# A recommendation tower on one core: TensorE raises its semaphores once for several results, and two looked-up features share a PSUM bank

## The chip, the cores and the metric

The kernel runs on one core of one Trainium2 chip. The metric is the device time of one launch in microseconds; the number given is the median of the runs. The engines are called as in the profile: PE (TensorE), PEld (its weight loads), DVE (VectorE), ACT (ScalarE), POOL (GpSimd) and SP (SyncE, which only issues transfers here).

## The reference, cut

2048 samples, 26 categorical features, vectors of 128 numbers.

```python
e = jnp.stack([tbl_f[ids[:, f]] for f in range(26)], axis=1)    # written out, feature by feature
combined = jnp.concatenate([dense[:, None, :], e], axis=1)       # 27 vectors a sample
interactions = jnp.einsum('bfd,bgd->bfg', combined, combined)
z = jnp.concatenate([dense, interactions[:, _IU0, _IU1]], axis=1)   # 128 + 351 pairs
h = jnp.concatenate([z, dense], axis=1)                          # 607
h = jnp.maximum(h @ W_top1 + b_top1, 0.0)                        # 607 -> 512
h = jnp.maximum(h @ W_top2 + b_top2, 0.0)                        # 512 -> 256
y = h @ W_top3                                                   # 256 -> 1
```

## The kernel before, in words

The batch is cut into 16 tiles of 128 samples, two tiles (`u` = 0 and 1) to a block `m`, 8 blocks (`LAST` = 7). Every engine runs its own hand-written program; semaphores alone set the order between them. Blocks 2 to 6 are a hardware loop, blocks 0, 1 and 7 are written out.

A block goes through these steps:

- **Gathers** (POOL, L372). For 18 of the features the 128 rows of a tile are fetched by one indirect DMA each, 18 in a row for a tile. They start when DVE has copied the tile's ids to `tile_ids` (L736), which it does in the middle of moving the tile before out of PSUM. The gathers for tile `u` of the next block therefore run while PE works on the dots of tile `u` of this one.
- **Look-ups** (`look_up_products`, L406). The other 8 features have 1000-row tables that stay in SBUF. DVE makes a one-hot matrix of 8 chunks for a feature and both tiles (`make_one_hots`, L723, `HOT` = 3 buffers), PE multiplies it with the table in a high and a low part: 16 matmuls of 256 columns for a feature, into bank `looked_up[n % 2]`. ACT copies the result out (L564, L566) and raises `product_copied`. PE raises `half_used` after 8 matmuls and `product_done` after 16; DVE refills the first half of a one-hot buffer after the one and the second half after the other.
- **Turns** (`turn_tile`, L427). 19 transposes of a tile in 5 groups, each group to a bank of its own, `turned_done` raised after each. DVE copies groups 0, 2, 4 (L739), ACT groups 1, 3 (L580).
- **Dots** (`dot_tile`, L445). 8 fills of 4 products each (8 matmul records a fill), in three banks in turn: fill `b` may start when fill `b` - 3 has been copied out. ACT copies each fill (L591) when `dots_done` says so. Below they are called fill 0 to fill 7; fills 2 and 5 go to the bank named `turned`.
- The dots go to DRAM and come back by pair (SP).
- **Layers**. Layer 1 has 4 outputs `o` of 12 matmuls (L465) in two banks; DVE adds the bias and applies the maximum (`relu_layer1`, L773), ACT and DVE split the result in a high and a low part. Layer 2 has 2 outputs of 12 matmuls (L498, L783), layer 3 is small (L508, L790). `layer_done` is raised after each output and once for layer 3.

PE's order in a steady block is: turn tile 0, layer 2 of two blocks ago, dots of tile 0, layer 3, the 8 look-ups for the next block, turn tile 1, output 0 of layer 1 of the block before, dots of tile 1, outputs 1 to 3. In the last block there are no look-ups and no gathers, and its own layer 1 goes to four banks (`last_layer1`, L483). In the first block, ACT makes the high part of table `n` + 3 only after it has copied feature `n` out.

Of the kernel before, what the change touches and what calls it, by code (L numbers as in the profile page):

```python
# [1 line left out]

# [8 lines left out]
P = 128  # L32
# [5 lines left out]
COLS = PER_BLOCK * P  # L38
# [4 lines left out]
LAYER1, LAYER2 = H1 // P, H2 // P  # L43
# [6 lines left out]
N_ROW, N_PRODUCT = len(ROW_FEATURES), len(PRODUCT_FEATURES)  # L50

SLOT_VECTORS = [0] + [f + 1 for f in ROW_FEATURES] + [f + 1 for f in PRODUCT_FEATURES]
PRODUCT_SLOT = 1 + N_ROW
TABLE_ROWS = 1000
CHUNKS = -(-TABLE_ROWS // P)
ROWS_K = TABLE_ROWS // CHUNKS
ROWS_SPRAY = ROWS_K - ROWS_K % 16
HOT = 3
# [9 lines left out]
N_GROUPS = len(GROUPS)  # L68
# [4 lines left out]
FILLS = QUADS // PER_BANK  # L73
# [8 lines left out]
K_TILES = 1 + PAIRS // K_PAIRS  # L82
SCRATCH_STORES = 2 * IN_QUAD
HIDDEN_LOADS = K_TILES - 1
WEIGHT_LOADS = 7
WEIGHT_SPLITS = 3
SPLIT_AFTER = 5

# [15 lines left out]
def build(nc, dense, ids, ids_by_feature, tables, W1, b1, W2, b2, W3, y):  # L104
    with ExitStack() as ctx:
# [10 lines left out]
        def sem(name):  # L116
            return ctx.enter_context(nc.semaphore(name))
# [8 lines left out]
        whole_tables, parts = sb_split("tables", [P, N_PRODUCT, CHUNKS, D])  # L126
# [3 lines left out]
        combined = sb("combined", [P, PER_BLOCK, P, VECTORS])  # L130
# [3 lines left out]
        ahead = sb("ahead", [P, N_PRODUCT, P])  # L134
# [66 lines left out]
        gathered = [[sem(f"gathered{u}_{g}") for g in range(N_GROUPS)] for u in range(PER_BLOCK)]  # L201
        dense_loaded = [sem(f"dense_loaded{u}") for u in range(PER_BLOCK)]
        one_hot_ready = sem("one_hot_ready")
        half_used = sem("half_used")
        product_done = sem("product_done")
        product_copied = sem("product_copied")
        ahead_moved = sem("ahead_moved")
# [19 lines left out]

        ids_by_tile = ids.rearrange("(p t) f -> p t f", t=TILES)
        dense_by_tile = dense.rearrange("(p t) d -> p t d", t=TILES)

        def tile_columns(ap, u):

# [159 lines left out]
        def _(pe):  # L392
            def look_up_products(m, first):

                for n in range(N_PRODUCT):

                    pe.wait_ge(one_hot_ready, m * N_PRODUCT + n + 1)
                    if first:

                        pe.wait_ge(table_split, n + 1)  # L400
                    if n >= 2:

                        pe.wait_ge(product_copied, m * N_PRODUCT + n - 1)
                    for c in range(CHUNKS):
                        for part in (HIGH, LOW):
                            last = nc.tensor.matmul(looked_up[n % 2][:, 0:COLS], parts[part][0:ROWS_K, n, c, :],  # L406
                                                    one_hot[0:ROWS_K, n % HOT, c, :],
                                                    start=(c == 0 and part == HIGH),
                                                    stop=(c == CHUNKS - 1 and part == LOW))
                        if c == CHUNKS // 2 - 1:  # L410
                            last.then_inc(half_used, 1)
                    last.then_inc(product_done, 1)

            def turn_tile(m, u, products, first=False):
                if not first:

                    pe.wait_ge(dots_copied, (m * PER_BLOCK + u) * FILLS)

                pe.wait_ge(dense_loaded[u], (m + 1) * 16)
                for g, slots in enumerate(GROUPS):  # L420
                    if g == 2:

                        pe.wait_ge(product_copied, products)

                    pe.wait_ge(gathered[u][g], (m + 1) * 16 * (len(slots) - (g == 0)))
                    for q, slot in enumerate(slots):
                        last = nc.tensor.transpose(group_bank[g][:, q * P:(q + 1) * P], rows[:, u, slot, :], identity[:])  # L427
                    last.then_inc(turned_done, 1)

            def dot_tile(m, u):  # L430

                pe.wait_ge(even_copied, (m * PER_BLOCK + u + 1) * EVEN_GROUPS)
                pe.wait_ge(odd_copied, (m * PER_BLOCK + u + 1) * ODD_GROUPS)
                if u == 0:
                    pe.wait_ge(product_copied, (m + 1) * N_PRODUCT)
                else:
                    pe.wait_ge(ahead_moved, m + 1)
                for b in range(FILLS):
                    if b >= DOT_BANKS:

                        pe.wait_ge(dots_copied, m * DOT_FILLS + u * FILLS + b - DOT_BANKS + 1)
                    for q in range(PER_BANK):
                        at = (b * PER_BANK + q) * IN_QUAD
                        quad = combined[:, u, at:at + IN_QUAD, :].rearrange("d j s -> d (j s)")
                        last = nc.tensor.matmul(dot_bank[b % DOT_BANKS][0:SQUARE, q * SQUARE:(q + 1) * SQUARE], quad, quad,  # L445
                                                start=True, stop=True)
                    last.then_inc(dots_done, 1)

            def layer1(n, first, outs=range(LAYER1)):

                pe.wait_ge(dense_kept, n + 1)
                if first:

                    pe.wait_ge(weights_split, WEIGHT_SPLITS)
                for o in outs:
                    if not first or o >= 2:

                        pe.wait_ge(layer_copied, n * LAYERS + max(0, o - 1))
                    for k in range(K_TILES):
                        if k > 0 and o == 0:  # L460

                            pe.wait_ge(pairs_split, n * HIDDEN_LOADS + k)
                        rows_k = P if k == 0 else K_PAIRS
                        for w, x in PART_PAIRS:
                            last = nc.tensor.matmul(mlp_bank[o % 2][:, 0:COLS], w1[w][0:rows_k, k, o * P:(o + 1) * P],  # L465
                                                    hidden0(x, rows_k, k), start=(k == 0 and w == x),
                                                    stop=(k == K_TILES - 1 and w == LOW))
                    last.then_inc(layer_done, 1)

            def last_layer1(tiles):  # L470

                if tiles[0] == 0:

                    pe.wait_ge(dense_kept, BLOCKS)
                    pe.wait_ge(dots_copied, BLOCKS * DOT_FILLS)
                for o in range(LAYER1):
                    for k in tiles:
                        if k > 0 and o == 0:

                            pe.wait_ge(pairs_split, LAST * HIDDEN_LOADS + k)  # L480
                        rows_k = P if k == 0 else K_PAIRS
                        for w, x in PART_PAIRS:
                            last = nc.tensor.matmul(last_bank[o][:, 0:COLS], w1[w][0:rows_k, k, o * P:(o + 1) * P],  # L483
                                                    hidden0(x, rows_k, k), start=(k == 0 and w == x),
                                                    stop=(k == K_TILES - 1 and w == LOW))
                    if tiles[-1] == K_TILES - 1:
                        last.then_inc(layer_done, 1)

            def layer2(n):

                pe.wait_ge(layer_copied, n * LAYERS + LAYER1 - 1)
                for o in range(LAYER2):
                    for k in range(LAYER1):
                        if o == 0:

                            pe.wait_ge(hidden1_split, n * LAYER1 + k + 1)
                        for w, x in PART_PAIRS:
                            last = nc.tensor.matmul(mlp_bank[o % 2][:, 0:COLS], w2[w][:, k, o * P:(o + 1) * P],  # L498
                                                    hidden1[x][:, k, :], start=(k == 0 and w == x),
                                                    stop=(k == LAYER1 - 1 and w == LOW))  # L500
                    last.then_inc(layer_done, 1)

            def layer3(n):

# [54 lines left out]
        def _(act):  # L559
            def copy_products(m, features=range(N_PRODUCT)):  # L560
                for n in features:

                    act.wait_ge(product_done, m * N_PRODUCT + n + 1)
                    nc.scalar.copy(combined[:, 0, :, PRODUCT_SLOT + n], looked_up[n % 2][:, 0:P])  # L564

                    nc.scalar.copy(ahead[:, n, :], looked_up[n % 2][:, P:COLS]).then_inc(product_copied, 1)  # L566

            def move_ahead(m, products):

# [125 lines left out]
        def _(dve):  # L695
# [8 lines left out]
            def make_one_hots(m, n, first):  # L704
# [10 lines left out]
                    dve.wait_ge(product_done, m * N_PRODUCT)  # L715
                for c in range(CHUNKS):
                    if n >= HOT and c == 0:

                        dve.wait_ge(half_used, m * N_PRODUCT + n - HOT + 1)
                    if n >= HOT and c == CHUNKS // 2:  # L720

                        dve.wait_ge(product_done, m * N_PRODUCT + n - HOT + 1)
                    last = nc.vector.tensor_scalar(one_hot[:, n % HOT, c, :], of,  # L723
                                                   chunk_row[:, c:c + 1], None, ALU.is_equal)
# [159 lines left out]
```

## Time and profile before

| | |
|---|---|
| median of 3 runs | 691.15 us (689.26 to 691.96) |
| span of the profiled execution | 677.5 us |
| outside the span, against the median | 13.65 us |
| PE busy | 423.8 us, 63% of the span |
| DVE, ACT, POOL busy | 239.6, 170.0, 275.0 us |
| matmuls | 2992 |
| gathers on POOL | 288, 273.7 us |

The page gives no time of its own for the profiled execution but the span, so the part outside it is counted against the median. Start times of PE's instructions are recorded; their ends are modelled. A release marked "remote" or "another core or an unknown queue" is one for which the profile found no instruction that ended just before: on one core, here, it means that the semaphore came long after the instruction that raises it had started.

### The profile page before, as it was taken

What the parts mean: (1) busy time and instruction counts of PE and PEld (TensorE: products, weight loads), DVE (VectorE), ACT (ScalarE), POOL (GpSimd) and SP (SyncE); (2) the same over time, 40 slices, a digit from 0 to 9 for tenths busy, and PEclk for the clock granted to TensorE, in tenths of its full rate; (3) what the DMA queues carried; (4) which work ended last, traced back from release to release, by engine and by line L of the source; (5) the groups of instructions that cost most, each with busy time, mean ns of one, the idle gap of its engine ahead of it and who ended that gap; (6) DMA issues with size and microseconds to landing.
All of it is one profiled execution on the core that took longest, in us unless ns stands there. A gap on an engine that the chain in (4) does not pass through costs nothing.

```text
span 677.5 us, 8517 instructions
## 1 busy us (share of the span) xinstructions
PE 423.8 (63%) x2992; PEld 403.1 (59%) x2992; DVE 239.6 (35%) x700; ACT 170.0 (25%) x366; POOL 275.0 (41%) x297
## 2 busy tenths in 40 slices
PE   2525354856947279471795726957269571784997
PEld 2415253855946179471794726956269471783997
DVE  5725210762504335043260432603434052530334
ACT  2204120431314024030231401313023040230551
POOL 6771737054172701727017271172712727036000
PEclk9967676786986659766597665976679575896899
DMA  8930211431114311243012430124301152001440
GB/s 222 275 93 14 71 31 50 83 108 43 51 52 83 90 29 44 55 86 87 15 48 53 81 92 12 54 51 81 94 28 48 52 99 74 19 23 50 85 64 23
DMA packets 61247, 46.01 MB, mean 68 GB/s; under 512 B 45677, under 2 KB 51301, under 8 KB 61228
## 3 DMA queue, kind: packets, MB, share of 16 engines
q1 hardware_dynamic: 52012, 26.87, 17.8%
q0 software_dynamic: 9216, 18.89, 10.8%
q8 instruction: 12, 0.20, 0.1%
q14 instruction: 7, 0.06, 0.0%
HBM read 37.20 MB, written 8.53 MB: 67 GB/s over the span
## 4 chain that ended last, share of the span: by engine, by line
PE 49%; another core or an unknown queue 34%; issue 11%; ACT 2%; DMA 2%; DVE 2%; SPq 1%; ACTq 0%; DVEq 0%
PE looked_up L406 20%; PE dot_bank L445 9%; PE mlp_bank L465 7%; PE mlp_bank L498 3%; PE turned L427 3%; PE turned L445 3%; PE looked_up L427 2%; DMA whole_tables<-in_tbl 2%; PE mlp_bank L508 1%; ACT dots L591 1%; PE dot_bank L427 1%; DVE whole_hidden L773 1%; ACT high_tables L635 1%; DVE combined L739 0%
## 5 line engine op out<-in xcount | busy, mean ns | idle before, releaser
L372 POOL DMA_INDIRECT rows<-in_tbl,tile_ids x288 | 273.7, 950 | 347.0 <-DVE tile_ids L736 262.4
L406 PE MATMUL looked_up<-one_hot,high_tables 125*128 125x256 f32 x512 | 144.0, 314 | 46.0 <-issue 23.4
L445 PE MATMUL dot_bank<-combined 128*108 128x108 f32 x768 | 99.4, 287 | 77.9 <-issue 41.8
L406 PE MATMUL looked_up<-one_hot,low_tables 125*128 125x256 f32 x512 | 141.6, 310 | 8.1 <-issue 8.1
L723 DVE TENSOR_SCALAR one_hot<-spread_ids,chunk_row 128x256 fp32r<-128x256 int32 x448 | 126.5, 359 | 52.6 <-remote 42.2
L406 PEld LDWEIGHTS looked_up<-one_hot,high_tables 125*128 125x128 f32 x512 | 113.0, 221 | 49.0 <-issue 49.0
L445 PEld LDWEIGHTS dot_bank<-combined 128*108 128x108 f32 x768 | 90.3, 197 | 84.1 <-issue 46.0
L406 PEld LDWEIGHTS looked_up<-one_hot,low_tables 125*128 125x128 f32 x512 | 112.7, 220 | 8.9 <-issue 8.9
L591 ACT COPY dots<-dot_bank 108x432 f32<-108x432 f32 x96 | 49.3, 519 | 242.3 <-remote 151.7
L773 DVE TENSOR_SCALAR whole_hidden<-mlp_bank,bias 128x256 f32<-128x256 f32 x28 | 13.5, 481 | 161.5 <-remote 99.1
L445 PE MATMUL turned<-combined 128*108 128x108 f32 x256 | 33.8, 281 | 47.2 <-issue 47.2
L445 PEld LDWEIGHTS turned<-combined 128*108 128x108 f32 x256 | 30.3, 194 | 48.2 <-issue 48.2
L564 ACT COPY combined<-looked_up 128x128 f32<-128x128 f32 x64 | 27.1, 423 | 118.4 <-PE looked_up L406 88.2
L465 PE MATMUL mlp_bank<-low_hidden,high_w 128*128 128x256 f32 (+1 forms) x112 | 40.4, 361 | 18.4 <-issue 18.4
L465 PEld LDWEIGHTS mlp_bank<-low_hidden,high_w 128*128 128x128 f32 (+1 forms) x112 | 29.1, 259 | 22.4 <-issue 22.2
L591 ACT COPY dots<-turned 108x432 f32<-108x432 f32 x32 | 16.6, 520 | 98.5 <-remote 85.5
L790 DVE COPY y_sb<-mlp_bank 128x2 f32 (+1 forms) x8 | 1.3, 159 | 112.8 <-PE mlp_bank L508 112.8
L465 PE MATMUL mlp_bank<-high_pairs,high_w 117*128 117x256 f32 x84 | 29.0, 346 | 13.3 <-issue 13.2
L465 PE MATMUL mlp_bank<-high_pairs,low_w 117*128 117x256 f32 x84 | 29.7, 354 | 10.2 <-issue 9.8
L427 PE MATMUL turned<-identity,rows 128*128 128x128 f32 x128 | 22.7, 337 | 13.8 <-ACT dots L591 13.8
L723 DVE TENSOR_SCALAR one_hot<-first_ids,chunk_row 128x256 fp32r<-128x256 int32 x64 | 19.8, 379 | 27.7 <-remote 20.8
L465 PEld LDWEIGHTS mlp_bank<-high_pairs,low_w 117*128 117x128 f32 x84 | 21.9, 261 | 12.0 <-issue 11.9
(73 smaller groups left out, 451.9 us busy)
## 6 DMA issues: line engine op xcount, KB each, us to landing
spread_ids<-in_ids_by_feature SPq DMA_DIRECT2D x28, 256.0 KB
scratch<-dots SPq DMA_DIRECT2D x28, 208.0 KB
rows<-in_tbl,tile_ids POOLq DMA_INDIRECT x288
whole_tables<-in_tbl SPq DMA_DIRECT2D x8, 448.0 KB
whole_hidden<-scratch SPq DMA_DIRECT2D x24, 117.0 KB
scratch<-dots SPq DMA_DIRECT2D x28, 52.0 KB
rows<-in_r_dense_features SPq DMA_DIRECT2D x16, 64.0 KB
first_ids<-in_ids_by_feature SPq DMA_DIRECT2D x1, 896.0 KB, 8.5
```

The lines of the kernel that those rows point to most:

```text
L372: nc.gpsimd.indirect_dma_start(rows[:, u, slot, :], None, tables[f][:, :], bass.IndirectOffsetOnAxis(ap=tile_ids[:, u, slot - 1:slot], axi ...
L406: last = nc.tensor.matmul(looked_up[n % 2][:, 0:COLS], parts[part][0:ROWS_K, n, c, :], one_hot[0:ROWS_K, n % HOT, c, :], start=(c == 0 and ...
L427: last = nc.tensor.transpose(group_bank[g][:, q * P:(q + 1) * P], rows[:, u, slot, :], identity[:])
L445: last = nc.tensor.matmul(dot_bank[b % DOT_BANKS][0:SQUARE, q * SQUARE:(q + 1) * SQUARE], quad, quad, start=True, stop=True)
L465: last = nc.tensor.matmul(mlp_bank[o % 2][:, 0:COLS], w1[w][0:rows_k, k, o * P:(o + 1) * P], hidden0(x, rows_k, k), start=(k == 0 and w == x),
L498: last = nc.tensor.matmul(mlp_bank[o % 2][:, 0:COLS], w2[w][:, k, o * P:(o + 1) * P], hidden1[x][:, k, :], start=(k == 0 and w == x), stop ...
L508: last = nc.tensor.matmul(mlp_bank[0][:, u:u + 1], hidden2[:, k, u, :], w3[:, k:k + 1], start=(k == 0), stop=(k == LAYER2 - 1))
L564: nc.scalar.copy(combined[:, 0, :, PRODUCT_SLOT + n], looked_up[n % 2][:, 0:P])
L591: nc.scalar.copy(dots[0:SQUARE, :, at:at + PER_BANK], dot_bank[b % DOT_BANKS][0:SQUARE, 0:PER_BANK * SQUARE].rearrange("p (q c) -> p c q", ...
L635: nc.scalar.copy(parts[HIGH][0:ROWS_K, n, :, :], whole_tables[0:ROWS_K, n, :, :]).then_inc(high_part_made, 1)
L723: last = nc.vector.tensor_scalar(one_hot[:, n % HOT, c, :], of, chunk_row[:, c:c + 1], None, ALU.is_equal)
L773: nc.vector.tensor_scalar(whole1[:, o, :], banks[o][:, 0:COLS], bias1[:, o:o + 1], 0.0, ALU.add, ALU.max).then_inc(layer_copied, 1)
```

## The change

No instruction is added, removed or moved on any engine. What changes is which matmuls raise a semaphore, by how much, and what waits for it:

- turns: `turned_done` is raised after group 1 (by 2) and after group 4 (by 3), no longer after each of the 5 groups;
- dots: `dots_done` is raised by 2 after every second fill (1, 3, 5, 7);
- look-ups: two features share a bank, in its two halves of 256 columns, so that the two banks hold four features. `product_done` is raised by 2 after the second of a pair. PE waits for `product_copied` once for a pair, and then for the pair two before. `half_used` is gone, and DVE waits for `product_done` ahead of the whole one-hot;
- layer 1: `layer_done` is raised by 2 after outputs 1 and 3; the last block's by 4 after output 3;
- layer 2: by 2 after output 1.

Every wait of ACT, DVE and SP keeps its count, so a waiter for the first of a pair now waits for the second. What order PE works in, the three banks of the dots and the three one-hot buffers stay.

```diff
+LOOKS_PER_BANK = 2
+TURNED_SIGNALS = {1: 2, N_GROUPS - 1: N_GROUPS - 2}
+DOTS_SIGNALS = {b: 2 for b in range(1, FILLS, 2)}
...
+        def look_view(n):
+            at = n % LOOKS_PER_BANK * COLS
+            return looked_up[n // LOOKS_PER_BANK % 2][:, at:at + COLS]
...
-                    if n >= 2:
-                        pe.wait_ge(product_copied, m * N_PRODUCT + n - 1)
+                    if n >= 2 * LOOKS_PER_BANK and n % LOOKS_PER_BANK == 0:
+                        pe.wait_ge(product_copied, m * N_PRODUCT + n - LOOKS_PER_BANK)
...
-                        if c == CHUNKS // 2 - 1:
-                            last.then_inc(half_used, 1)
-                    last.then_inc(product_done, 1)
+                    if n % LOOKS_PER_BANK == LOOKS_PER_BANK - 1:
+                        last.then_inc(product_done, LOOKS_PER_BANK)
...
-                    last.then_inc(turned_done, 1)
+                    if g in TURNED_SIGNALS:
+                        last.then_inc(turned_done, TURNED_SIGNALS[g])
...
-                    last.then_inc(dots_done, 1)
+                    if b in DOTS_SIGNALS:
+                        last.then_inc(dots_done, DOTS_SIGNALS[b])
...
-                    last.then_inc(layer_done, 1)
+                    if o % 2 == 1:
+                        last.then_inc(layer_done, 2)
...
-                    if tiles[-1] == K_TILES - 1:
-                        last.then_inc(layer_done, 1)
+                if tiles[-1] == K_TILES - 1:
+                    last.then_inc(layer_done, LAYER1)
...
-                    last.then_inc(layer_done, 1)
+                last.then_inc(layer_done, LAYER2)
...
                 for c in range(CHUNKS):
                     if n >= HOT and c == 0:
-                        dve.wait_ge(half_used, m * N_PRODUCT + n - HOT + 1)
-                    if n >= HOT and c == CHUNKS // 2:
                         dve.wait_ge(product_done, m * N_PRODUCT + n - HOT + 1)
```

ACT's copies of the look-ups (L564, L566) read `look_view(n)` instead of `looked_up[n % 2]`.

## Rows read from the trace of the kernel before

**Rows 1.** The page: its head.

```profile
span 677.5 us, 8517 instructions
```

**Rows 2.** Waits: who waited for whom; us in total, times, longest.

```profile
ACT dots L591 <- remote: 237.2, 38, 14.2
...
DVE whole_hidden L773 <- remote: 99.1, 4, 24.9
```

**Rows 3.** Timeline, dots of tile 0: start, us, engine, what [idle before <- releaser].

```profile
216.80 0.94 POOL L372 DMA_INDIRECT rows<-in_tbl,tile_ids  x1 [11.44 <-DVE tile_ids L736]
...
220.00 1.91 PE L445 MATMUL dot_bank<-combined 128*108 128x108 f32 x16
...
228.93 0.52 ACT L591 COPY dots<-turned 108x432 f32<-108x432 f32 x1 [8.07 <-remote]
...
238.03 0.94 POOL L372 DMA_INDIRECT rows<-in_tbl,tile_ids  x1 [0.31 <-issue]
238.05 0.52 ACT L591 COPY dots<-dot_bank 108x432 f32<-108x432 f32 x1 [8.61 <-remote]
...
242.26 0.52 ACT L591 COPY dots<-dot_bank 108x432 f32<-108x432 f32 x1 [3.70 <-remote]
```

**Rows 4.** Timeline, dots of tile 1 and outputs 1 and 2 of layer 1.

```profile
352.79 0.94 POOL L372 DMA_INDIRECT rows<-in_tbl,tile_ids  x1 [29.50 <-DVE tile_ids L736]
...
353.09 0.48 DVE L773 TENSOR_SCALAR whole_hidden<-mlp_bank,bias 128x256 f32<-128x256 f32 x1 [0.65 <-PE mlp_bank L465]
...
359.04 1.01 PE L445 MATMUL dot_bank<-combined 128*108 128x108 f32 x8 [1.42 <-issue]
...
361.92 1.77 PE L445 MATMUL dot_bank<-combined 128*108 128x108 f32 x8 [1.87 <-issue]
...
366.08 0.41 PE L465 MATMUL mlp_bank<-high_dense,high_w 128*128 128x256 f32 x1
...
367.01 0.35 PE L465 MATMUL mlp_bank<-low_hidden,high_w 128*128 128x256 f32 x1 [0.52 <-issue]
...
368.45 0.52 ACT L591 COPY dots<-turned 108x432 f32<-108x432 f32 x1 [6.58 <-remote]
...
373.99 0.94 POOL L372 DMA_INDIRECT rows<-in_tbl,tile_ids  x1 [0.30 <-issue]
...
377.59 0.52 ACT L591 COPY dots<-dot_bank 108x432 f32<-108x432 f32 x1 [8.63 <-remote]
...
378.26 0.37 PE L465 MATMUL mlp_bank<-high_pairs,low_w 117*128 117x256 f32 x1
...
378.49 0.48 DVE L773 TENSOR_SCALAR whole_hidden<-mlp_bank,bias 128x256 f32<-128x256 f32 x1 [24.91 <-remote]
```

**Rows 5.** Timeline, the end of the dots of tile 0, two blocks later.

```profile
405.01 1.78 PE L445 MATMUL turned<-combined 128*108 128x108 f32 x8 [11.69 <-issue]
...
412.17 0.94 ACT L591 COPY dots<-dot_bank 108x432 f32<-108x432 f32 x2 [7.22 <-remote]
...
412.74 3.22 PE L445 MATMUL dot_bank<-combined 128*108 128x108 f32 x16 [5.96 <-ACT dots L591]
```

**Rows 6.** The chain that ended last: start, us, what.

```profile
379.03 2.93 PE mlp_bank L465 x12
...
583.27 15.46 PE looked_up L406 x128
...
667.93 2.17 PE dot_bank L483 x18
671.00 2.64 PE mlp_bank L498 x18
```

**Rows 7.** Timeline, DVE in the look-ups: half a one-hot.

```profile
249.80 1.14 DVE L723 TENSOR_SCALAR one_hot<-spread_ids,chunk_row 128x256 fp32r<-128x256 int32 x4 [0.56 <-PE looked_up L406]
```

**Rows 8.** Timeline, DVE in the turn of tile 1.

```profile
436.28 0.69 DVE L739 COPY combined<-looked_up 128x512 f32<-128x512 f32 x1 [0.18 <-PE looked_up L427]
...
437.18 0.17 DVE L736 COPY tile_ids<-all_ids 128x18 int32 x1 [0.21 <-PE dot_bank L427]
```

More of the change, by code:

```diff
@@ L203, in build @@
         one_hot_ready = sem("one_hot_ready")
-        half_used = sem("half_used")
         product_done = sem("product_done")
@@ L400, in look_up_products @@
                         pe.wait_ge(table_split, n + 1)
-                    if n >= 2:
-                        pe.wait_ge(product_copied, m * N_PRODUCT + n - 1)
+                    if n >= 2 * LOOKS_PER_BANK and n % LOOKS_PER_BANK == 0:
+                        pe.wait_ge(product_copied, m * N_PRODUCT + n - LOOKS_PER_BANK)
                     for c in range(CHUNKS):
                         for part in (HIGH, LOW):
-                            last = nc.tensor.matmul(looked_up[n % 2][:, 0:COLS], parts[part][0:ROWS_K, n, c, :],
+                            last = nc.tensor.matmul(look_view(n), parts[part][0:ROWS_K, n, c, :],
                                                     one_hot[0:ROWS_K, n % HOT, c, :],
@@ L563, in copy_products @@
                     act.wait_ge(product_done, m * N_PRODUCT + n + 1)
-                    nc.scalar.copy(combined[:, 0, :, PRODUCT_SLOT + n], looked_up[n % 2][:, 0:P])
-                    nc.scalar.copy(ahead[:, n, :], looked_up[n % 2][:, P:COLS]).then_inc(product_copied, 1)
+                    nc.scalar.copy(combined[:, 0, :, PRODUCT_SLOT + n], look_view(n)[:, 0:P])
+                    nc.scalar.copy(ahead[:, n, :], look_view(n)[:, P:COLS]).then_inc(product_copied, 1)
             def move_ahead(m, products):
```

## The prediction

> **What bounds the kernel now.** I read the page first. The span is 677.5 us [rows 1] and PE, the busiest engine, works 63% of it, so a third of the time is waiting. The table of waits says where: ACT waits 38 times, 237.2 us in all, for the fills of the dots, and DVE 4 times, 99.1 us, for an output of layer 1 [rows 2]. Both wait for PE, and both rows say "remote": the semaphore came long after the matmul. So the next view is the timeline of the places where that happens.
>
> Tile 0 of a block: the gathers of POOL start at 216.80. PE starts the last matmuls of fills 3 and 4 from 220.00 and is through with them by 221.91. ACT receives fill 2 at 228.93, fill 3 at 238.05, fill 4 at 242.26. The last of the 18 gathers starts at 238.03 and ends at 238.97 [rows 3]. So while POOL gathers, PE's semaphores come up to 16 us late and some 9 us apart; 3.3 us after the last gather everything owed arrives at once. Tile 1 shows the same: gathers from 352.79 to 374.93, fill 5 received at 368.45, fill 6 at 377.59, although fills 6 and 7 were issued at 359.04 and 361.92 [rows 4].
>
> The question on which all hangs is what is slow: the semaphore, or every instruction of PE. Output 2 of layer 1 answers it. Its 12 matmuls run from 366.08 to 378.26, 12.2 us, where 12 of the same take 2.93 us in output 3 [rows 4, 6]. Eleven of these twelve raise no semaphore, and they wait for none. They do not come in bursts after a semaphore is let through; the second already waits 0.52 us for nothing that is seen [rows 4]. At 366.08 what PE has issued and not been acknowledged is fill 6, fill 7 and output 1, 8 + 8 + 12 matmuls, each with its weight load: 56 instructions, and the rest of fill 5. I read that as a queue of a fixed length, emptied in order at one rate for every instruction: the 16 instructions of fill 6 take 377.59 - 368.45 = 9.1 us, 0.57 us each; the 24 of output 2 take 12.2 us, 0.51 us each. The rate goes with the instruction, not with the semaphore.
>
> So each of the stretches is pinned at both ends: it starts with the gathers, and ends some 3 us after them, plus what is still to do then. There are 14 of them, two in each of blocks 0 to 6.
>
> **The change part by part.** Fewer semaphores do not shorten that queue, since all 2992 matmuls and their loads remain. What they do is to let waiters start later.
>
> *Output pairs of layer 1.* Now output 0 is received at 353.09, before the queue is full; bank 0 is free, and output 2 is done under the stretch's cover, so only output 3 is left at 379.03 [rows 4, 6]. After the change output 0 is told of together with output 1, at 378.49. Output 2 then waits for the bank and comes behind the stretch. It costs the time of 12 matmuls, 2.93 us less what of that is waiting [rows 6]; what is late next is the turn of tile 0, its copies, and through `tile_ids` the gathers. I take 2.4 us, six times (blocks 1 to 6): 14.4 us. Bounds: 0 if some other stretch swallows it, 2.9 us each, 17.4 us.
>
> *Fill pairs, tile 0.* Fill 5 needs fill 2 copied. Before, fill 2 is received ahead of the end and fill 5 runs at 405.01; fills 6 and 7 follow at 412.74 and take 3.22 us [rows 5]. After it, fill 2 is received with fill 3, at 412.17, and three fills of 1.6 us stand there instead of two: +1.6 us. Where fill 3 is received before the end, as at 238.05, fill 7 is held by fill 4 at 242.26 as before, and the cost is 0 [rows 3]. In the trace four of the five looped blocks look like the first case. I take 1.2 us, six times: 7.2 us; bounds 0 and 1.6 us each, 9.6 us. Tile 1 has the same waits, but there PE has outputs 1 and 2 to do under cover: 0.
>
> *Turns, tile 1.* Groups 2, 3 and 4 are told of together. DVE now copies group 2 at 436.28, while PE transposes, and `tile_ids` at 437.18 [rows 8]; after it, group 2 (0.69 us) comes first, so `tile_ids` and all 18 gathers start 0.65 us later, and the stretch ends that much later. Six times: 3.9 us. For tile 0 DVE is behind PE with its own work already: 0.
>
> *Look-ups.* PE takes 15.46 us for 128 matmuls, 1.93 us a feature [rows 6]; DVE makes half a one-hot in 1.14 us, some 2.1 us for a whole one when it does not stop [rows 7]. So DVE is the slower one, and only the three one-hots in store hide it. Before, it starts the fourth after half of feature 0, at about 1.0 us; 5 x 2.1 us later, at 11.5, the last is ready, and PE wants it at 13.5: hidden. After it, DVE starts the fourth only when features 0 and 1 are done, at 3.9 us; the last is ready at 3.9 + 5 x 2.1 = 14.4, and with the semaphores between at about 14.5: PE ends at 16.4 instead of 15.46, +1.0 us, and +1.2 where its clock is low at first. I take 1.1 us, six times: 6.6 us; bounds 0 and 1.9 us each (DVE at its slower rate beside gathers), 11.4 us. The wider banks take PE's wait for ACT's copies away; in the steady blocks it is not seen, so nothing is gained. In the first block they let feature 4 run early, but feature 5 then waits for its one-hot, which waits for features 2 and 3 together; both ways end after the gathers. I count 0, and 2.5 us for the two stretches of block 0 and the later copies.
>
> *The last block.* There are no gathers. Its layer 1 gives up all four outputs at once: DVE's four maxima of 0.48 us [rows 4] stand behind the last matmul instead of beside them, between 667.93 + 2.17 and 671.00 [rows 6]: about +1.4 us. The copy of fill 6, the wait of output 2 for output 0's maximum and layer 2's pair add 0.4, 0.65 and 0.65 us. Sum 3.1 us; bounds 1 and 5 us.
>
> *The semaphores themselves.* 128 matmuls with 16 raises among them are 0.121 us apart [rows 6], so a raise costs no time that I can see outside the stretches: 0. The Trainium skill (TensorE: Matmul & The Clock Gate, section "The cost: per-tile semaphore tail") speaks for the change: increments serialize, and each adds 26.3 ns. No row here shows it. By that rule alone the 233 raises removed (64 in the dots, 48 in the turns, 96 in the look-ups, 25 in the layers) would give back 6.1 us, and the time would be 685 us if nothing else happened.
>
> The sum is 14.4 + 7.2 + 3.9 + 6.6 + 2.5 + 3.1 = 37.7 us. The span becomes 715.2 us; with the 13.65 us outside it, 728.9 us: I say 729. All low bounds together give some 698 us, all high ones some 741 us.
>
> **The rivals.**
>
> *The semaphore is what is slow (faster).* If each raise is held up while POOL gathers, and the instructions only behind it, then half the raises are half the waiting. For it: the 38 waits of ACT come one by one with a fill, 6.2 us each [rows 2], and so does what the change removes. Against it: output 2, which crawls without raising anything [rows 4]. Price: 38 x 6.2 / 2 = 119 us back, less the 37.7 us: 691 - 119 + 38 = 610 us. It decides as soon as fill 3 is received some 9 us earlier than now.
>
> *The semaphore is slow, but the end of the stretch is set by the gathers (little change).* Then tile 0 ends with fill 7 already done, 5 us less in each of six blocks instead of 7.2 us more, but the other terms stay: 729 - 7 - 21 = 701 us.
>
> *The page's rule, with the losses hidden (slightly faster).* As a mechanism of this kernel: every later start of ACT and DVE falls into a wait that POOL sets anyway, output 2 included, and only the work around raises is saved. By rows this is bounded by 0 us: 691 us. With the rule of the skill (the section named above) it is 685 us.
>
> *The first block goes wrong (slower still).* ACT makes tables 5 to 7 only after a pair is received. If the pair of features 4 and 5 misses the burst after the gathers, or the signals come later by one more stretch of 9 us [rows 3], that is 9 us or more on top, 738 to 750 us.
>
> **How the numbers follow.** My forecast, with its own range 705 to 742, has 0.67; the first rival 0.13; the second 0.07; the third 0.08 (half of it faster, half within 0.5%); the fourth 0.05. The range 690 to 746 leaves out the first rival, part of the third and part of the fourth, together just under 0.2. Half a per cent is about what a measurement of this kernel can tell from no change. Faster: 0.13 + 0.04 and a little for what I don't see, 0.18. Same: 0.04 and the edge of the second, 0.06. Slower: 0.76.
>
> **What the profile after would show.** ACT's waits for the dots: four a tile, longer each, with the total near 237 us or above (right), or near half (first rival). The time from the last gather to the next burst stays 3 us. Behind it stand 24 matmuls of L465 in the chain instead of 12. The look-ups of a block take 16.5 to 18.5 us instead of 15.5 to 17.4, with DVE named as the releaser. `tile_ids` of tile 1 comes after a copy of 0.69 us. The prediction is wrong if outputs of layer 1 or fills are received while the gathers still run, in shorter steps than 9 us; then my reading of the queue has fallen.

## The result and the profile after

The changed kernel is slower: 721.8 us against 690.7 us, ratio 1.048 (95% interval 1.042 to 1.055). Two further sets gave 1.054 (1.048 to 1.061) and 1.055 (1.053 to 1.058). The range held, the direction and the size too: the sum was +37.7 us, and by their ratios the three sets show +33, +37 and +38 us.

One number of mine was wrong and cancels out. A run's time is its span and 1.8 us (731.26 us for a span of 729.5 us), not 13.65 us more. The profile of before, with a span of 677.5 us, stands for a run of 679.3 us: 1.7% below the median of 690.7 us, and below the lowest of the six runs behind it (684.5 us). As a ratio of spans the forecast was 715.2 / 677.5 = 1.056.

The page of the changed kernel, its head (answers to [rows 1]) and its waits (answers to [rows 2]):

```profile
span 729.5 us, 8489 instructions
...
PE 421.7 (58%) x2992; PEld 399.8 (55%) x2992; DVE 236.7 (32%) x700; ACT 160.7 (22%) x366; POOL 275.4 (38%) x297
```

```profile
ACT dots L581 <- remote: 284.8, 28, 21.0
DVE whole_hidden L760 <- remote: 156.5, 6, 26.1
```

ACT waits less often for the dots and longer in all: 28 times and 284.8 us, where it was 38 and 237.2. In a second profile of the changed kernel it is 26 times and 271.3 us. Half the raises did not halve the waiting. The work is the same, 2992 matmuls, and what was added is idle time. The two spans differ by 52 us, but only some 31 to 38 us of that are the change's: the profiled execution of the changed kernel was the slowest of its six runs, and that of before was a short one. The table by stages below therefore has further profiles beside these two.

Tile 1, the end of a stretch of the changed kernel (timeline; answers to [rows 4]):

```profile
399.76 0.94 POOL L359 DMA_INDIRECT rows<-in_tbl,tile_ids  x1 [0.30 <-issue]
404.06 0.94 ACT L581 COPY dots<-dot_bank 108x432 f32<-108x432 f32 x2 [11.74 <-remote]
404.18 0.88 DVE L760 TENSOR_SCALAR whole_hidden<-mlp_bank,bias 128x256 f32<-128x256 f32 x2 [26.02 <-remote]
404.72 0.58 PE L453 MATMUL mlp_bank<-high_dense,high_w 128*128 128x256 f32 x1 [8.41 <-DVE whole_hidden L760]
```

and the chain that ended last, the same place (answers to the first of [rows 6]):

```profile
404.72 5.44 PE mlp_bank L453 x24
```

The last gather ends at 400.70; 3.4 us later ACT gets fills 6 and 7, and DVE gets outputs 0 and 1 together. Behind the stretch stand 24 matmuls and 5.44 us, where 12 and 2.93 us stood. That step happened as told, in every block.

Tile 0 (timeline; answers to [rows 3] and [rows 5]):

```profile
415.06 0.94 POOL L359 DMA_INDIRECT rows<-in_tbl,tile_ids  x1 [14.35 <-DVE tile_ids L723]
...
426.51 0.52 ACT L581 COPY dots<-turned 108x432 f32<-108x432 f32 x1 [8.85 <-remote]
...
440.68 0.52 ACT L581 COPY dots<-dot_bank 108x432 f32<-108x432 f32 x1 [13.22 <-remote]
441.09 0.53 ACT L581 COPY dots<-turned 108x432 f32<-108x432 f32 x1
...
443.06 0.94 ACT L581 COPY dots<-dot_bank 108x432 f32<-108x432 f32 x2 [1.45 <-PE dot_bank L432]
```

Here I was wrong. Fill 3 comes with fill 2 at 11.4 us after the first gather, not at the burst, so fill 6 too is issued ahead of it, and only fill 7 is left behind it. The copy of the last fill starts 28.4 us after the first gather, where it was 29.4 in the block of [rows 5].

The look-ups (timeline of DVE, one block; answers to [rows 7]), ahead of them the same of the kernel before:

```profile
422.49 8.50 DVE L723 TENSOR_SCALAR one_hot<-spread_ids,chunk_row 128x256 fp32r<-128x256 int32 x32 [0.20 <-PE looked_up L406]
```

```profile
449.89 4.30 DVE L710 TENSOR_SCALAR one_hot<-spread_ids,chunk_row 128x256 fp32r<-128x256 int32 x16 [5.03 <-PE looked_up L393]
454.36 4.29 DVE L710 TENSOR_SCALAR one_hot<-spread_ids,chunk_row 128x256 fp32r<-128x256 int32 x16 [0.17 <-PE looked_up L393]
458.82 2.19 DVE L710 TENSOR_SCALAR one_hot<-spread_ids,chunk_row 128x256 fp32r<-128x256 int32 x8 [0.17 <-PE looked_up L393]
```

Before, DVE makes four one-hots in one run. After, it makes two, stops, and is let go by PE 4.46 us later each time: a one-hot (2.19 us) and the feature that uses it and completes the pair (2.18 us on its own) now stand in a row.

The turn of tile 1 (timeline; answers to [rows 8]) goes as forecast, group 2 and then the ids:

```profile
465.72 0.69 DVE L726 COPY combined<-looked_up 128x512 f32<-128x512 f32 x1 [0.88 <-PE dot_bank L413]
466.33 0.17 DVE L723 COPY tile_ids<-all_ids 128x18 int32 x1
```

**By stages.** The table is made from the timelines: from the first matmul of a stage to the first of the next, mean of blocks 2 to 6, in us. "More raises" is an experiment below whose time is that of before; it shows how far one profile differs from the next. Its block is 85.12 us and lies nearer to the usual run of before than the 83.76 us of the short profile.

| | turn 0 | layer 2 | dots 0 | layer 3 | look-ups | turn 1 | output 0 | dots 1 | outputs 1-3 | block |
|---|---|---|---|---|---|---|---|---|---|---|
| before | 3.25 | 2.95 | 27.23 | 1.37 | 16.68 | 2.00 | 1.51 | 10.45 | 18.32 | 83.76 |
| more raises (e9) | 2.96 | 2.95 | 27.92 | 1.60 | 17.23 | 1.99 | 1.51 | 12.93 | 16.04 | 85.12 |
| after | 2.08 | 2.95 | 28.46 | 1.45 | 18.83 | 2.37 | 1.77 | 15.72 | 15.77 | 89.40 |
| after, again | 2.09 | 2.96 | 27.84 | 1.60 | 18.70 | 2.37 | 1.76 | 15.56 | 16.04 | 88.91 |

Dots 1 and outputs 1 to 3 belong together: 28.8 and 29.0 us before, 31.5 and 31.6 after.

### The profile page after: what moved, and what is told of

Its sections match the earlier page's. It is cut to its first block, busy times and chain, and to the rows that moved or that the text cites. A ratio compares the mean times of both kernels' runs of the same rounds, so it can differ in the third digit from the quotient of the medians.

```text
span 729.5 us, 8489 instructions
## 1 busy us (share of the span) xinstructions
PE 421.7 (58%) x2992; PEld 399.8 (55%) x2992; DVE 236.7 (32%) x700; ACT 160.7 (22%) x366; POOL 275.4 (38%) x297
## 4 chain that ended last, share of the span: by engine, by line
another core or an unknown queue 42%; PE 34%; DVE 10%; issue 8%; ACT 3%; DMA 2%; SPq 1%; DVEq 0%; ACTq 0%
PE looked_up L393 13%; DVE one_hot L710 7%; PE dot_bank L432 6%; PE mlp_bank L453 5%; PE mlp_bank L488 3%; PE looked_up L413 2%; ACT dots L581 2%; PE turned L432 1%; PE mlp_bank L498 1%; DMA first_ids<-in_ids_by_feature 1%; PE turned L413 1%; DVE low_tables L691 1%; PE dot_bank L413 1%; DVE whole_hidden L760 1%
## 5 line engine op out<-in xcount | busy, mean ns | idle before, releaser
L393 PE MATMUL looked_up<-one_hot,high_tables 125*128 125x256 f32 x512 | 146.0, 317 | 45.5 <-DVE low_tables L691 22.6
L432 PE MATMUL dot_bank<-combined 128*108 128x108 f32 x768 | 101.2, 290 | 97.0 <-ACT dots L581 56.5
L393 PEld LDWEIGHTS looked_up<-one_hot,high_tables 125*128 125x128 f32 x512 | 111.1, 217 | 54.8 <-issue 44.1
L393 PEld LDWEIGHTS looked_up<-one_hot,low_tables 125*128 125x128 f32 x512 | 110.9, 217 | 9.2 <-issue 9.2
L581 ACT COPY dots<-dot_bank 108x432 f32<-108x432 f32 x96 | 46.8, 522 | 259.5 <-remote 201.9
L432 PE MATMUL turned<-combined 128*108 128x108 f32 x256 | 35.6, 289 | 89.2 <-issue 69.0
L760 DVE TENSOR_SCALAR whole_hidden<-mlp_bank,bias 128x256 f32<-128x256 f32 x28 | 12.9, 480 | 179.8 <-remote 156.5
L453 PE MATMUL mlp_bank<-high_dense,high_w 128*128 128x256 f32 x28 | 12.9, 462 | 50.5 <-DVE whole_hidden L760 50.5
L453 PEld LDWEIGHTS mlp_bank<-high_dense,high_w 128*128 128x128 f32 x28 | 7.6, 272 | 52.4 <-DVE whole_hidden L760 52.4
L453 PEld LDWEIGHTS mlp_bank<-low_hidden,high_w 128*128 128x128 f32 (+1 forms) x112 | 31.0, 277 | 0.0
L453 PE MATMUL mlp_bank<-high_pairs,high_w 117*128 117x256 f32 x84 | 30.5, 363 | 0.0
```

Of the source, the lines that this page charges most:

```text
L393: last = nc.tensor.matmul(look_view(n), parts[part][0:ROWS_K, n, c, :], one_hot[0:ROWS_K, n % HOT, c, :], start=(c == 0 and part == HIGH), ...
L581: nc.scalar.copy(dots[0:SQUARE, :, at:at + PER_BANK], dot_bank[b % DOT_BANKS][0:SQUARE, 0:PER_BANK * SQUARE].rearrange("p (q c) -> p c q", ...
L760: nc.vector.tensor_scalar(whole1[:, o, :], banks[o][:, 0:COLS], bias1[:, o:o + 1], 0.0, ALU.add, ALU.max).then_inc(layer_copied, 1)
```

## The experiments

The theory: while POOL gathers, what PE has finished is acknowledged late, in order, at a rate for each instruction; the end of such a stretch is set by the gathers; the change moves work out of its cover and starves PE of one-hots. The main rival: a raise is what is slow.

### One part at a time

Layer pairs alone (e1), fill pairs alone (e2), the look-ups alone (e3), the turns alone (e4). Before took 688.2 us beside them.

```diff
e1:  -                    last.then_inc(layer_done, 1)
     +                    if o % 2 == 1:
     +                        last.then_inc(layer_done, 2)      # last_layer1: LAYER1 at the end; layer2: LAYER2 at the end
e2:  -                    last.then_inc(dots_done, 1)
     +                    if b % 2 == 1:
     +                        last.then_inc(dots_done, 2)
e3:  look_view, the wait for product_copied by pairs, product_done by pairs, no half_used
e4:  -                    last.then_inc(turned_done, 1)
     +                    if g in (1, N_GROUPS - 1):
     +                        last.then_inc(turned_done, 2 if g == 1 else N_GROUPS - 2)
```

> The kernel before with the layer pairs alone (layer 1 after outputs 1 and 3, layer 2 after output 1, the last block's layer 1 after output 3). My theory (a queue at a rate per instruction, stretches pinned to the gathers): output 2 of layer 1 comes out of cover, some 2.4 us a block in blocks 1 to 6 (14.4 us) and 2.7 us at the end, so 17 us more, about +2.5%, and 24 matmuls instead of 12 behind each stretch of tile 1. Rival (a raise is what is slow while POOL gathers): fewer raises ahead of the burst, so 5 us or more less than before.

> The kernel before with the fill pairs of the dots alone. As predicted: +1.2 us a block in six blocks, +7 us (+1.0%). What the trace of the changed kernel suggests instead: nothing a block (28.6 against 28.7 us from the first gather to the end of the dots of tile 0), so within 3 us of before. Rival (a raise is slow): half the raises are half the waiting, 30 us or more less.

> The kernel before with the look-ups of the change alone (two features in a bank, product_done by pairs, no half_used). As predicted: DVE's later start costs 1.1 us a block, +6.6 us (+1.0%). The trace of the changed kernel suggests 2.15 us a block, +13 us (+1.9%), DVE the releaser of every second feature. Rival (raises are slow): 16 raises fewer 4 in a stage without gathers change nothing; in the first block they save up to 9 us.

> The kernel before with the turns raised twice alone. As predicted: tile_ids and with it the gathers of tile 1 start 0.65 us later in six blocks, +3.9 us (+0.6%). The trace of the changed kernel suggests 0.83 us for tile 1 and 0.16 for tile 0: +6 us (+0.9%). Rival: nothing, or a little less than before.

| part | predicted | ratio (95%) | us |
|---|---|---|---|
| e1 layer pairs | +17 | 1.012 (1.005 to 1.020) | +8.5 |
| e2 fill pairs | +7 | 1.006 (1.002 to 1.010) | +4.0 |
| e3 look-ups | +6.6 | 1.025 (1.021 to 1.030) | +17.4 |
| e4 turns | +3.9 | 1.008 (1.004 to 1.012) | +5.6 |
| sum | +34.5 | | +35.5 |

No part makes the kernel faster, and the four add up to the whole (+33 to +38 us). The rival wanted at least one below before. The look-ups cost most, not the layers: their +17.4 us is above both numbers that were expected of them, 6.6 and 13 us, and the +8.5 us of the layer pairs is half of the 17 expected.

In e1 each stretch of tile 1 has 5.17 us behind it on average instead of 2.73, +2.4 us a block; but in two of its five looped blocks the dots of tile 0 took 22.9 and 22.2 us, where the other three took 27.7 to 28.7 and before took 26.2 to 28.0. In these two, fill 4 is received at 20.7 and 20.0 us after the first gather, ahead of the burst at 25.6, and PE is through with fill 7 at 23.0 and 22.3 us. That gives back some 10 us in the profiled run and fits a rise by half of what I added up; the other runs of e1 have no profile, so it is not shown for them. Why the acknowledgements came sooner in these two blocks isn't known.

In e3 the look-ups took 18.59 us a block. Its profiled run, 696.7 us, was the shortest of its four (median 704.6 us), so about 8 us of the +17.4 are in no profile that I have.

### More raises, without and with stretches

Four raises a fill instead of one: three of them on a semaphore that nobody waits for.

```diff
+                        if q < PER_BANK - 1:
+                            last.then_inc(extra_raised, 1)
                     last.then_inc(dots_done, 1)
```

> The kernel before with four raises a fill instead of one: each of the first three products of a fill raises a semaphore that nobody waits for. My theory (the late queue goes by instructions): the fills are received as before, 24 raises more a tile cost under 3 us in all, ratio 1.00. Rival (a raise is what is slow while POOL gathers): fills 2 to 5 are received later by several us each, and the time is 10 us or more above before.

The set in which this ran, on another chip, held a surprise: the kernel before took 406.8 us there, not 688. No stretches, not one "remote" wait for the dots. More raises: ratio 1.000 (0.998 to 1.003), and 6.10 us for the dots of tile 0 where the same stage without the extra raises took 6.08 beside gathers (e8, below) and 6.07 without them (e6). So it was repeated in a set where before took 687.2 us:

> Four raises a fill instead of one again, beside the run above. Without stretches it was level with before (0.03 us a tile). If this set has the stretches: my theory (the late queue goes by instructions) says that the fills are received as in the kernel before and the dots of tile 0 end 27 to 29 us after the first; the rival (a raise is slow there) says that fills 2 to 4 are received several us later each and that the time is over 10 us above before.

Ratio 1.000 (0.994 to 1.007). Its fills in a stretch of tile 0 (timeline of ACT and POOL):

```profile
389.58 0.94 POOL L373 DMA_INDIRECT rows<-in_tbl,tile_ids  x1 [11.99 <-DVE tile_ids L739]
...
395.47 0.52 ACT L594 COPY dots<-dot_bank 108x432 f32<-108x432 f32 x1 [3.43 <-remote]
...
406.80 0.52 ACT L594 COPY dots<-turned 108x432 f32<-108x432 f32 x1 [10.81 <-remote]
415.25 0.94 ACT L594 COPY dots<-dot_bank 108x432 f32<-108x432 f32 x2 [7.93 <-remote]
```

Fill 2 is received 17.2 us after the first gather and fills 3 and 4 at 25.7, with 24 more raises in the tile; in the kernel before, in the block of [rows 5], it is 17.9 and 25.6. Over the five looped blocks fill 2 is received 16.0 us after the first gather on average, and 16.1 us in the kernel before; fill 3 at 24.5 and 24.4. The number of raises does not set the rate. The rival is out. Outside the stretches 24 raises cost 0.03 us at most, about 1 ns each. The Trainium skill (TensorE: Matmul & The Clock Gate, "The cost: per-tile semaphore tail") gives 26.3 ns a raise, from a fit on small matmuls that run side by side in the array. Carried over to these matmuls, which follow each other, it would be an estimate of 0.63 us here; this case's trace does not show it, and the measurement decides.

But it is not one rate either. In the kernel before, the 16 instructions between the receipt of fill 1 and that of fill 2 of tile 0 take 8.5 to 14.8 us in the five looped blocks, 0.53 to 0.92 us each. What goes with a soon or a late receipt of fill 3 is when PE starts the dots of tile 0, counted from the first gather (looped blocks, read from the timelines; for pairs, the receipt of fills 2 and 3 together):

| | raises a fill | dots start, us | fill 3 received, us |
|---|---|---|---|
| before | 1 | 0.9 to 1.5 | 21.3 to 25.7 |
| more raises (e9) | 4 | 0.7 to 1.0 | 20.6 to 25.9 |
| look-ups (e3), two late blocks | 1 | 1.3 and 1.5 | 25.7 and 24.9 |
| look-ups (e3), three early blocks | 1 | -0.1 to 0.3 | 15.6 to 19.2 |
| turns (e4) | 1 | 0.4 to 1.0 | 17.2 to 24.9 |
| layer pairs (e1) | 1 | -0.1 to 0.2 | 10.8 to 25.1 |
| fill pairs (e2), four late blocks | 1 for two | 0.5 to 1.0 | 20.6 to 24.8 |
| fill pairs (e2), one early block | 1 for two | 0.2 | 11.5 |
| changed kernel, three profiles | 1 for two | -0.1 to 0.3 | 8.6 to 25.7 |

In 19 of the 24 blocks with an early start (up to 0.3 us after the first gather), fill 3 comes at 9 to 19 us, with one raise a fill and with one for two alike; after a later start it comes at 17 to 26 us. No run changes the start alone, so this is a correlation, and the width of the early rows stays unexplained.

### Without the gathers

The gathers of blocks 1 to 7 are left out; their tiles are computed from the rows of block 0.

```diff
-                for g, slots in enumerate(GROUPS):
+                for g, slots in enumerate(GROUPS if first else []):
...
-                    pe.wait_ge(gathered[u][g], (m + 1) * 16 * (len(slots) - (g == 0)))
+                    pe.wait_ge(gathered[u][g], 16 * (len(slots) - (g == 0)))
```

> The kernel before without the gathers of blocks 1 to 7 (their tiles are computed from the rows of block 0, so part of the gathering is left out); everything else, DVE's copies of the ids too, stays. My theory: the gathers are what makes PE's semaphores late, so no wait of ACT for a fill is longer than 2 us after the first block, the period of a block falls from 84 to some 50 us and the span to some 470 us. Rival (the late semaphores come from something else, the stores and loads of SP for instance): the stretches stay, over 600 us.

> The changed kernel without the gathers of blocks 1 to 7 (left out as in the run above). My theory: what the pairs cost apart from the gathers stays, that is the look-ups (1 to 2 us a block) and short waits for pairs in the dots and layer 1 (1 to 2 us a block): 10 to 25 us above the kernel before without gathers. Rival (the loss is one of the congested stretches alone): within 5 us of it.

> The kernel before without the gathers of blocks 1 to 7 (left out; their tiles are computed from the rows of block 0), again. In a set without stretches it took 368.9 us, 41.17 us a block. If this set has the stretches (before at 688 us): my theory (the gathers bring them) says 41 to 42 us a block here too, and about 375 to 390 us in all; the rival (something else of this set makes PE's semaphores late) says that waits of 5 us and more stay in the dots of blocks 1 to 6, over 500 us.

e6 and e7 ran in the set without stretches: 368.9 and 403.1 us; e10 in a set with them, where before took 689.6 us: 394.3 us, ratio 0.572 (0.569 to 0.575). e6 was expected at some 470 us and took far less. e10 lies a little above the 375 to 390 us expected: of its 25.4 us over e6, 24.2 are spent before the first turn of block 0 (at 64.3 instead of 40.1 us), where the gathers remain. The waits of e10 (who waited for whom; us, times, longest):

```profile
ACT dots L591 <- PE dot_bank L445: 55.5, 96, 3.3
DVE whole_hidden L773 <- PE mlp_bank L465: 55.0, 15, 7.5
...
ACT combined L564 <- remote: 33.4, 3, 26.6
```

No "remote" wait for a fill or an output is left. The one of 26.6 us is in block 0. Blocks 2 to 6 take 41.17 us each in both sets, to the hundredth. So the stretches need two things: gathers on POOL, and a chip that shows them. What the second thing is no run tells.

Without gathers the change can be read with nothing around it:

| | turn 0 | layer 2 | dots 0 | layer 3 | look-ups | turn 1 | output 0 | dots 1 | outputs 1-3 | block |
|---|---|---|---|---|---|---|---|---|---|---|
| before (e6) | 1.99 | 2.95 | 6.07 | 0.83 | 15.43 | 1.99 | 1.51 | 6.01 | 4.38 | 41.17 |
| after (e7) | 1.99 | 2.96 | 6.41 | 0.83 | 17.29 | 2.38 | 1.76 | 6.36 | 5.23 | 45.21 |

4.04 us a block, of which the look-ups are 1.86, outputs 1 to 3 are 0.85 (output 2 waits for output 0's maximum), the dots 0.69, the turn and output 0 are 0.64. Over the whole run it is 34.2 us, above the 10 to 25 us expected and as much as with the stretches; the price is nearly the same, though paid elsewhere. Why the two sums are so close no run tells.

### Two features in a bank, but DVE told as before

```diff
-                        if c == CHUNKS // 2 - 1:
+                        if c == CHUNKS // 2 - 1 or c == CHUNKS - 1 and n % LOOKS_PER_BANK == 0:
                             last.then_inc(half_used, 1)
...
+                        k = n - HOT     # first half: half_used; second half: half_used or, for odd k, product_done
```

> The look-ups of the change (two features in a bank, ACT told by pairs), but DVE is told of each half and each feature as before. My theory (the one-hots are what comes late): the loss of the look-ups alone, 2.5%, goes to under 0.5%, and the stage takes 15.5 to 17.5 us again. Rival (the pair of copies of ACT behind the last look-up, or the shared bank): over half of the loss stays.

It ran in the set without stretches: 406.0 us, ratio 0.998 (0.995 to 1.001). The ratio alone proves little there, since POOL's gathers set the time; the chain that ended last says so:

```profile
by line: POOL rows L378 66.0%; issue 24.1%; PE mlp_bank L472 1.7%; PE mlp_bank L505 1.2%; PE dot_bank L452 1.1%; PE looked_up L490 0.8%; PE dot_bank L490 0.7%; DMA rows<-in_tbl,tile_ids 0.6%; DMA all_ids<-in_ids 0.5%; PE mlp_bank L515 0.5%;
```

The stage decides: its look-ups take 15.81 us a block, beside gathers; in e5, with the look-ups of before, 15.89; with the change's own it is 17.29 even without gathers (e7). So the shared bank and ACT's pairs are innocent in this stage, and the one-hots were what came late. In a set with the stretches this version did not run. The 2.37 us of turn 1 stay: there PE waits for both copies of the last pair.

### The changed kernel twice more

> The changed kernel once more, since the kernel before took 688 us beside the first four experiments and 407 us beside the next four. If the kernel before takes 407 us here (no stretches): PE's own path without gathers grew from 41.2 to 45.2 us a block, and POOL needs 45 us a block for 36 gathers, so the two paths are about level; with DVE slower beside the gathers I expect 47 to 49 us a block and 425 to 435 us, ratio 1.05 to 1.07. Rival (POOL's path hides the loss): 407 to 412 us. If the kernel before takes 688 us: the ratio of 1.048 again.

> The changed kernel a third time. If the kernel before takes 407 us beside it (no stretches), I expect 47 to 49 us a block and 425 to 435 us, ratio 1.05 to 1.07; the rival, that POOL's path of 45 us a block hides the loss, gives 407 to 412 us. If the kernel before takes 688 us: a ratio between 1.042 and 1.061, as in the two sets before.

Both sets had the stretches: 727.1 us against 687.2, and 728.7 us against 689.6. What the change does to the time of a set without stretches was not measured. PE's 45.2 us a block and POOL's 45 (36 gathers 1.25 us apart) would be level there; I expected 425 to 435 us, and that stays an expectation.

## Why the prediction held, point by point

- **A rate for each instruction, not for each raise.** Right in what decided the forecast: four times the raises changed nothing, in sets with and without stretches. One rate of 0.51 to 0.57 us an instruction it is not; between fills 1 and 2 of tile 0 it is 0.53 to 0.92 us. And the receipts of [rows 3] were read too low: fill 4, issued by 221.91, is received at 242.26, 20 us late and not 16.
- **The sign of being wrong.** The prediction called itself wrong if fills were received during the gathers in steps shorter than 9 us. Taken by the letter this came: in the profile of the changed kernel the pairs of one tile are received 1.7, 4.3 and 12.9 us after the first gather. The kernel before has such steps too (2.8, 7.1 and 15.6 us in the last looped block), so the sign could not tell the rivals apart. Four raises a fill could.
- **Stretches pinned to the gathers.** Right for tile 1: the burst comes 3.3 to 3.4 us after the last gather, in before and after alike, and without gathers there is none. For tile 0 mostly; in two of e1 PE was through with the dots 0.1 and 0.8 us after the last gather, ahead of the burst. What I didn't see is that the gathers alone don't make them: one chip ran the same kernel in 406.8 us.
- **Layer pairs, 14.4 us.** The mechanism right, 2.4 us a block behind the stretches of tile 1; the part alone cost 8.5 us, last block included, because two stretches of tile 0 were shorter in its profile.
- **Fill pairs, 7.2 us.** The wrong step is that fill 3 would be received only with the burst. It came 11.5 to 17.3 us after the first gather in the second profile of the changed kernel and 10 to 26 us after it in the first, mostly ahead of the burst. So the dots of tile 0 end 28.6 and 28.0 us after the first gather on average, where it was 28.7 us; before, only three of the five blocks had fill 3 with the burst, and not four as the prediction has it. Alone, in e2, the pair came 11.5 to 24.8 us after the first gather, and the part cost 4.0 us. The pair comes sooner in the changed kernel than fill 3 did (21 to 26 us) without need of fewer raises: with one raise a fill, e1 and e3 have it as soon where PE starts the dots as early. The prediction had no term for that start, which moved from about 1 us behind the first gather to level with it (turn 0 took 2.1 us instead of 3.25).
- **Turns, 3.9 us.** Right in its mechanism; 5.6 us alone. To the 0.65 us comes that PE itself waits for DVE's later copies before the dots: 1.76 us from output 0 to the dots instead of 1.51.
- **Look-ups, 6.6 us.** The mechanism right, the size wrong, 17.4 us. The term was sized with 1.93 us a feature, PE's pace without a stop; between two stops it is 2.18 us, and each of three pairs waits so. That makes 1.9 us a block instead of 1.1. The pair's copies by ACT add 0.4 us at turn 1, which the sum left out. Six times 2.3 us are 14 us; the rest isn't accounted for.
- **First block, 2.5 us.** Too low: the turn of block 0 starts at 67.8 to 68.1 us in three profiles of the changed kernel, against 61.7 us in before and 63.9 us in more raises; with 64.0 us in e1 and e2 too, that is some 4 us.
- **Last block, 3.1 us.** All four maxima of DVE do stand behind the last matmul. The chain there (answers to the last of [rows 6]):

```profile
717.36 2.17 PE dot_bank L473 x18
...
722.44 2.63 PE mlp_bank L488 x18
```

2.9 us lie between them, where 0.9 us did: +2.0 us where I had taken 1.4.

- **The second rival's price.** It was put at 701 us, from 729 - 7 - 21. Its own terms, 5 us less in each of six blocks, give 729 - 7 - 30 = 692 us. That changes nothing in what was measured.

The errors of the parts had both signs (layers and fills too high, turns, look-ups and first block too low), and their sum was right to a few us. That is partly luck.

## What to carry to other kernels

A semaphore raised once for two results makes the first result as late as the second. It costs nothing only where every waiter has work or a buffer in store for that long. Count the store (three one-hots, two banks) before merging raises. And before taking a late semaphore for an expensive one, look at instructions that raise nothing: if they crawl too, the number of raises is not the cause. Adding raises is the cheap test of it.

## What the runs showed of the hardware

- Each set of runs has one chip. The kernel before took 404 to 409 us (21 runs) on one chip and 683 to 695 us (34 runs) in three sets on others. The granted clock follows: 0.95 to 0.98 on the one with all gathers in place, 0.74 to 0.79 on the others.
- In the sets with stretches PE's acknowledgements come late while POOL issues indirect DMAs: in the kernel before ACT receives a fill up to 21 us after its last matmul has started. Counted from a fill's last matmul to the last one issued before ACT receives that fill, matmuls and weight loads together, 64 instructions are outstanding at most, in each of the profiles of before, e1, e3, e4 and e9. In [rows 4] fills 6 and 7 and output 1 with their loads are 56 of them. Where PE is held so, it goes on at 0.51 us an instruction (output 2 in [rows 4]).
- What differs between the chips is not settled; whether the recording of instructions, which is on in all these profiles, has a part in it, is not either. POOL itself issues at 1.25 us a gather in both.
- 24 more raises on 64 matmuls cost 0.03 us at most, about 1 ns a raise.
